# A split of weights moved into attention, a plan fetched early, and longer runs of unread products, in a four-layer kernel on one Trainium2 core

## What is computed

```python
def _routed_moe(x, gate_w, w0, w1, wo):
    logits = jnp.einsum('td,de->te', x, gate_w)
    top_logits, top_idx = jax.lax.top_k(logits, K)          # K = 2 of E = 8 experts
    top_w = jax.nn.softmax(top_logits, axis=-1)
    cw = jnp.zeros((T, E), dtype=x.dtype).at[jnp.arange(T)[:, None], top_idx].add(top_w)
    out = jnp.zeros_like(x)
    for e in range(E):
        h = jax.nn.silu(x @ w0[e]) * (x @ w1[e])            # 512 -> 1024
        out = out + cw[:, e:e + 1] * (h @ wo[e])            # 1024 -> 512
    return out
...
x = x + _L0_xattn_ref(_layernorm(x, axis=-1), ...)
x = x + _L0_ffn_ref(_layernorm(x, axis=-1), ...)
x = x + _L1_xattn_ref(_layernorm(x, axis=-1), ctx_512, ctx_512)   # 32 heads of 16, 8 of keys and values
x = x + _L1_ffn_ref(_layernorm(x, axis=-1), L1_ffn_gate_w, L1_ffn_w0, L1_ffn_w1, L1_ffn_wo, ...)
```

## Time and profile before

| | |
|---|---|
| median of 3 runs | 1661.46 us (1660.38 to 1663.22) |
| the profiled execution | 1661.82 us |
| its span, first to last instruction | 1659.9 us |
| busy: TensorE | 1567.9 us (94%) |
| busy: VectorE, ScalarE, GpSimd | 947.7, 715.4, 701.0 us |
| attention of the second layer | about 490 to 905 us |
| experts | about 939 to 1659 us |

### The profile page before, as it was taken

One profiled execution on the slowest core, in us unless ns is written; L12 is line 12 of the kernel. 1 busy time (PEld: TensorE's weight loads), 2 busy tenths in 40 slices (PEclk: granted clock), 3 DMA queues, 4 the chain that ended last, 5 costly groups with the idle time before them and its releaser, 6 DMA issues.

```text
span 1659.9 us, 24705 instructions
## 1 busy us (share of the span) xinstructions
PE 1567.9 (94%) x8251; PEld 1050.8 (63%) x8278; DVE 947.7 (57%) x1539; ACT 715.4 (43%) x1166; POOL 701.0 (42%) x479
## 2 busy tenths in 40 slices
PE   6879999999989999999998799999999999999998
PEld 4565657565653333434333788788788888788886
DVE  6998979797888898988884522222222222222221
ACT  5885645455546777767776211111111111111111
POOL 1224261534513125353464756561771170930064
PEclk9889999999999999999999999999999999999999
DMA  9189800000231455343531615322340231530088
GB/s 354 70 305 386 291 1 1 1 1 1 85 94 45 121 138 150 92 129 109 150 105 55 213 69 178 125 78 70 146 177 31 83 127 28 188 127 26 26 141 214
DMA packets 90946, 196.18 MB, mean 118 GB/s; under 512 B 7154, under 2 KB 9075, under 8 KB 90227
## 3 DMA queue, kind: packets, MB, share of 16 engines
q1 hardware_dynamic: 71746, 156.68, 28.3%
q0 software_dynamic: 7168, 17.04, 4.6%
q10 hardware_dynamic: 11952, 21.43, 3.9%
HBM read 113.28 MB, written 81.32 MB: 117 GB/s over the span
## 4 chain that ended last, share of the span: by engine, by line
PE 69%; DVE 15%; POOL 6%; ACT 3%; DMA 3%; issue 3%; another core or an unknown queue 0%; SPq 0%; POOLq 0%; DVEq 0%; ACTq 0%
PE psum L2962 11%; PE psum L2964 11%; PE psum L2963 11%; PE psum L2605 7%; PE psum L2816 6%; PE psum L2805 5%; DVE neg_max L2081 4%; POOL expert_weight_parts L1070 3%; PE psum L2650 3%; PE psum L2779 3%; PE psum L2620 2%; DMA w_of_even_expert<-in_L_ffn_w 2%; PE psum L2986 2%; POOL expert_weight_parts L1069 1%; DVE inner_rotated_t_second L1945 1%
## 5 line engine op out<-in xcount | busy, mean ns | idle before, releaser
L2081 DVE TENSOR_REDUCE neg_max<-psum 128x2 f32<-128x1024 f32 x248 | 291.9, 1220 | 43.1 <-PE psum L2779 40.8
L1440 ACT ACTIVATE probabilities<-psum 128x512 f32<-128x512 f32 x512 | 269.8, 604 | 82.0 <-PE psum L2805 77.8
L2223 DVE TENSOR_TENSOR expert_inner<-psum,expert_inner 128x512 f32<-128x512 f32 x78 | 53.9, 691 | 390.2 <-ACT expert_inner L1545 390.2
L2962 PE MATMUL psum<-expert_weight_parts,sorted_tokens_t_first 128*128 x624 | 251.3, 403 | 9.0 <-POOL expert_weight_parts L1070 5.3
L2963 PE MATMUL psum<-expert_weight_parts,sorted_tokens_t_first 128*128 x624 | 247.5, 397 | 0.0
L2964 PE MATMUL psum<-expert_weight_parts,sorted_tokens_t_second 128*128 x624 | 247.4, 396 | 0.0
L1545 ACT ACTIVATE expert_inner<-psum 128x512 f32<-128x512 f32 x78 | 46.6, 598 | 397.9 <-PE psum L2964 397.9
L2805 PE MATMUL psum<-query_rows,key_rows 50*128 50x512 f32 x512 | 183.0, 449 | 5.8 <-ACT probabilities L1440 2.1
L2779 PE MATMUL psum<-key_rows,query_rows 48*128 48x512 f32 x496 | 176.2, 483 | 7.1 <-DVE neg_max L2081 3.3
L2962 PEld LDWEIGHTS psum<-expert_weight_parts,sorted_tokens_t_first 128*128 128x128 f32 x624 | 118.2, 189 | 37.6 <-issue 11.0
L2816 PE MATMUL psum<-probabilities,value_and_one 128*32 128x512 f32 x1024 | 139.3, 617 | 1.5 <-ACT probabilities L1440 0.9
(11 more groups left out here) (316 smaller groups left out, 2972.9 us busy)
## 6 DMA issues: line engine op xcount, KB each, us to landing
sorted_x<-zero_rows SPq DMA_DIRECT2D x9, 3960.0 KB, 30.7
w_of_odd_expert<-in_L_ffn_w SPq DMA_DIRECT2D x8, 2048.0 KB
wo_of_expert<-in_L_ffn_wo SPq DMA_DIRECT2D x7, 2048.0 KB, 8.5
query_rows<-query_rows_of_units SPq DMA_DIRECT2D x64, 192.0 KB, 3.6
w_of_even_expert<-in_L_ffn_w SPq DMA_DIRECT2D x6, 2048.0 KB, 11.6
sorted_tokens<-sorted_x ACTq DMA_DIRECT2D x39, 264.0 KB, 2.7
sorted_y<-expert_out ACTq DMA_DIRECT2D x39, 256.0 KB, 2.1
query_rows_of_units<-dims_first SPq DMA_DIRECT2D x32, 256.0 KB
```

What stands on the lines that cost most here:

```text
L1440: nc.scalar.activation(prob[t % 2][:, i * SEQ:(i + 1) * SEQ], ring(("score", n)), ACT.Exp, scale=HD ** -0.5).then_inc(c_e, 1)
L2081: nc.vector.tensor_reduce(of_pair[:, p, st, :], ring(("max", (m, i))).rearrange("p (h n) -> p h n", h=2), AX.X, ALU.max, negate=True).then ...
L2223: nc.vector.tensor_tensor(h, bank[2 * half + 1], h, ALU.mult).then_inc(e_h, 1)
L2962: nc.tensor.matmul(out_bank, hi[:, cols], w_r[:, bass.ds(w_at, 512)], start=start, stop=False)
```

## The change

GpSimd: both halves of w1 are now split in unit 29, behind the addition of unit 28. A wait is added that the third batch's logits have been picked, since the first part is written over the buffers of that batch's normed values and logits. The two splits in unit 30 and in phase d are gone. TensorE: the unread runs of phase d grow from 8 to 14 and from 50 to 70, and 12 are added behind the first tile's transposes. The three numbers of the second tile's plan are read at the end of the first tile's products and kept in registers.

```diff
@@ GpSimd, phase_c
-                    if u == UNITS - 2:
-                        half_split(w_in_raw[0][1], W_IN[0][1], 0, w_in_parts, 0)
+                    if u == UNITS - 3:
+                        pool.wait_ge(d_lgp, BATCH - 1)
+                        for h in range(2):
+                            half_split(w_in_raw[0][1], W_IN[0][1], h, w_in_parts, h)
@@ GpSimd, phase_d
                 last_scatters()
-                half_split(w_in_raw[0][1], W_IN[0][1], 1, w_in_parts, 1)
                 pool.wait_ge(*scattered(2))
@@ TensorE, phase_d
                 pick(BATCH - 1)
-                unread(8)
+                unread(14)
                 rank(BATCH - 1)
-                unread(50)
+                unread(70)
                 pe.wait_ge(*scattered(BATCH - 1))
                 unread(10)
+                known = {}
+
+                def places(i):
+
+                    return ([pe.value_load(plan[0:1, bass.ds(5 * i + w, 1)], min_val=0, max_val=max(W_IN[0][w], W_IN[1][w]))
+                             for w in range(2)], first_of_expert(i))
@@ TensorE, step(i, parity)
-                    at = [pe.value_load(plan[0:1, bass.ds(5 * i + w, 1)], min_val=0, max_val=max(W_IN[0][w], W_IN[1][w]))
-                          for w in range(2)]
-                    first_step = first_of_expert(i)
+                    at, first_step = known.pop(1) if static(i) and i == 1 else places(i)
...
                         last.then_inc(e_gu, 1)
+                    if static(i) and i == 0:
+                        known[1] = places(1)
                     if not static(i) or i + 1 < MTILES:
                         transpose_x(i + 1, 1 - parity)
@@ TensorE, ahead of the tiles
                 transpose_x(0, 0)
+                unread(12)
                 tile_loop(pe, step)
```

## The result

The changed kernel takes **1671.75 us** (median of 4 runs, 1670.75 to 1672.79), the kernel before 1660.92 (4 runs, 1659.87 to 1663.22): a ratio of **1.0056**, 95% interval 1.0039 to 1.0073. In a later set of runs the same pair gave 1662.28 against 1656.38, ratio 1.0034 (1.0011 to 1.0057). The profiled execution took 1672.17 us, its span is 1670.3, against 1659.9: 10.4 us to account for.

The account below looks back on a forecast made before the run. TensorE's waits were taken to bound the kernel, here between the last attention units and the first expert's products. First product +2.1, early plan -1.4: +0.7, 1662.5 us on the profile, 1662.2 beside the median; range 1656.8 to 1665.8.

Parts of the forecast that it names:

- What the removal gives: Taking the half split from ahead of the last addition brings the last batch's choice 4.1 us sooner.
- The block at 879.99: VectorE's tensor_tensor with two SBUF inputs blocks until GpSimd's moved subtraction ends at 884.1; TensorE's score group starts 4.0 us late.
- rival B: VectorE isn't blocked at 879.99, so the split's move gives -4.1 us and the kernel takes 1657.2; chance 0.18.
- The clock behind it: After 4.9 us idle ahead of the score group, TensorE runs about 3 us at half speed, costing 1.1 (bounds 0 and 2).
- rival C: Half speed after the 4.9 us idle lasts until attention ends, costing 7.7 us in place of 1.1: 1668.8; chance 0.09.
- Sum of part 1: Net effect of moving the splits, at the choice of the last batch: +0.9 us.
- The long run ahead of the tile: Unread products overrun the last scatter's landing by 2.0 us; the first tile's transposes come at 937.9, +1.2.
- Twelve behind the transposes: Twelve unread products between the first tile's transposes and its first product cost +0.9 us (to +2.4).
- The early plan: Reading the second tile's plan behind the first tile's products removes the issue wait ahead of 954.05: -1.4 us.
- Behind 955 us no list is changed: From the second tile on instruction lists stay the same, and GpSimd's earlier next splits are worth 0.
- Rival D: Clock falls again ahead of the tile; ten unread products cost 4.1 us, not 2.3: 1664.0; chance 0.73 together with main forecast.
- behind 943, part 2 was mis-sized: Sign: a first product later than 943 us (forecast 941.1) would show the longer unread runs were mis-sized.

Follow-up runs that it names:

- e1: The kernel before with only the split change: both half splits in unit 29, none ahead of the last addition or behind the last scatters; 1660.32 us, ratio 1.0014.
- e5: The changed kernel with 15 unread products on TensorE in the idle stretch ahead of the score group that waits for blocked VectorE; one run, 1655.16 us.
- e4: The changed kernel with the third batch's comparison at about 880 made by four tensor_scalar operations in place of one tensor_tensor; 1665.72 us, ratio 1.0037.
- e6: The kernel before with the early second-tile plan, and the half split ahead of the last addition moved behind the third batch's choice; 1653.17 us, ratio 0.9967.
- second profile: The changed kernel profiled once more, with nothing altered; units 28 to 29 took 19.58 us, and the kernel measured 1662.28 us in that set.
- e9: The changed kernel with 48 more TensorE instructions, waits already met, at the start of attention; 1665.81 us, ratio 1.0055.
- e11: The changed kernel with 104 more TensorE instructions, repeats of waits already met, spread over the first stage; 1661.89 us, ratio 1.0021.
- e7: The kernel before with only the 12 unread products behind the first tile's transposes; one run, 1658.46 us.
- e8: The kernel before with only the longer unread run, 70 products in place of 50; 1658.33 us, ratio 1.0001.
- e2: The kernel before with only the unread runs changed: 14, 70 and 12 products in place of 8, 50 and 0; 1661.86 us, ratio 1.0025.

## Why the prediction was wrong

By its own steps:

- **What the removal gives.** I had 4.1 us at the choice (2.9 idle, 0.9 clock, 0.3 power). e1: 4.2. Right.
- **The block at 879.99.** 4.0 us, then the second comparison until the second subtraction ends: 4.03 and 4.36. Right, in place and size; rival B is out. For attention it costs 4.5 (e5), within the 4.0 to 4.6 that I gave. That the cause is two inputs was too narrow (e4, e6); what it is, the runs don't show.
- **The clock behind it: the step that failed.** I took the fall to last about 3 us, as in both stretches of the earlier trace rows, let 0.9 of them pass idle and came to 1.1, bounds 0 and 2. In the changed kernel the clock read 0.50 or 0.51 from 885 until 894 and 0.79 from 894 to 897, and 0.50 from 876 to 891 in its second profile. e5 prices it at 3.3 us up to the sums of unit 29, three times my term. The attended sums of unit 29 come 7.6 to 7.9 us later in place of 5.1. The mechanism was that of rival C, at about half its size; I had weighed it with 0.09 and left it out of the range. Behind the idles of the earlier trace rows stood router and unread products, here attention: I read a duration off places that were not alike. Whether that is why it lasted longer is open. Behind the block it lasts about 10 us (e1, e9, e11, the first profile) or 17 (e4, the second profile), but in the same attention, without the block's idle ahead of it, it lasts about 3 in e5, e7, e8 and e9, and about 10 from 872 us in the first profile.
- **Sum of part 1**, +0.9: measured +3.65 (e1), +5.5 in the changed kernel's two profiles. Of the 2.75 that e1 is over my sum, 2.2 are the clock (3.3 for 1.1) and 0.5 the block. The 1.9 from e1 to the changed kernel are, in the second profile, 1.9 more between units 29 and 30, where the half clock of the block goes on; e4 has the same. In the first they are 1.5 between units 30 and 31, where a copy of ScalarE starts 1.0 us late for a reason that I can't see, and 0.7 behind that, with the clock down once more (0.56 from 912 to 915), less 0.4 ahead of them. Neither is in e1, e9 or e11. What the first profile adds is in no other, and I don't count it as the change's; the longer half clock follows the block in two of the six traces that have it, so it may be.
- **The long run ahead of the tile.** I had the 140 passes overrun the landing by 2.0 and cost 1.2. They overrun it by 0.9 and cost nothing (e8: -0.1): the 12.3 us that I read for 100 passes held an issue wait of 0.76 us. What costs 1.7 to 2.2 is a fetch of instructions on top of the last scatter's packets (e2, e9, e11), for which I had no term. The recorded profile is a case apart: its fetch starts 20.3 us behind the choice, and the 2.3 us are in the three issue waits, 0.70 + 1.03 + 1.03. No q8 packet lies near them: one ends 9 us ahead of the first, the next starts 2.4 us behind the last. The kernel before has one like the first at the same place (0.76, behind 98 passes), and none of the other twelve traces has any. Their cause is open.
- **Twelve behind the transposes**, +0.9: measured 1.14 to 1.22, the plan's fetch hidden under them but for 0.23 to 0.28 us (in the first profile its three loads start at 946.05, 946.92 and 947.57, under the 24 passes from 945.36 to 948.20).
- **The early plan**, -1.4: measured -1.5, nothing given back.
- **"Behind 955 us no list is changed"**: true of the lists, and I priced it at 0. It was +1.35 and +0.9 up to the eighth tile. The load of the third expert's weights costs 1.2 more where a fetch falls into it, and e11 gives that back.
- **Rival D** (the longer runs don't keep the clock): no. The ten behind the wait ran at full speed, the first tile too (granted clock 1.00 from 938 to 954). (With the 70 alone, in e8, the first tile did not.)
- My tell-tale "behind 943, part 2 was mis-sized" was met (948.43), but part 1 had by then failed by more.

For the changed kernel's second profile the corrected terms are +5.5 (sums 28 to the choice), +1.7, +1.2, -1.5 and +0.9: 7.8 us. The two recorded ratios, 1.0056 and 1.0034, are 9.3 and 5.6 us of 1661 and 1656.

## What to carry to other kernels

Ahead of moving work into another engine's idle time, look at what each neighbour executes in that time, not at whether it is on the path: two operations of 0.2 us turned into 8.4. When you price a fall of the clock, take half speed for the whole rest of the stage as the upper bound, as rival C had it: in one and the same attention it lasted anywhere from 3 to 17 us. And filler isn't free even where its time is hidden: it is instructions, and they shift the fetches behind it (the 104 of e2 one from 29.73 to 16.98 us behind the choice, onto the last scatter). Compare stretches in two profiled executions before you believe a total of a few us.

## What the runs showed of the hardware

- A tensor_scalar from SBUF to SBUF is blocked by GpSimd's subtraction, and in e4 by its copy too (four of 8 columns took 6.09 us, one of 4 columns took 3.84 in e6). A reduction (0.18 us in e4) and an operation with one operand in PSUM (0.42 us in e6) are not.
- A 16 KB packet of instructions (0.9 to 1.9 us) that meets the last packets of a scatter makes it land 1.7 to 2.3 us later; inside a load of two 2 MB transfers it costs about 1.2. The first is gone with 48, 60 or 104 more instructions of TensorE ahead of it (e9, e5, e11), the second with 104 (e11). How the packet holds up the scatter the traces don't show.
- TensorE's clock fell once from 872 us on in code that no variant changed (1.9 us), and at a lower price in four other traces (0.6 to 1.5 us). I know no cause.
